# attention_2: transposes of the probability rows three units behind the scores instead of two

## What is computed

```python
x = layer_norm(image_embeds, ln1_g, ln1_b)      # 32 context tokens
l = layer_norm(latents, ln2_g, ln2_b)           # 512 tokens
q = l @ Wq
kv = jnp.concatenate([x, l], axis=1) @ Wkv      # 544 keys and values
w = jax.nn.softmax(einsum('bhqd,bhkd->bhqk', q * scale, k * scale), axis=-1)
out = einsum('bhqk,bhkd->bhqd', w, v)
return out @ Wo
```

## Time and profile before

| | |
|---|---|
| median of three executions | 2352.45 us (2346.61 to 2354.46) |
| profiled execution | 2344.8 us, of which the span is 2343.0 us |
| TensorE matmul busy | 1963.6 us (84%) |
| TensorE weight loads busy | 1245.7 us (53%) |
| VectorE, ScalarE, GpSimd busy | 1222.7 us (52%), 927.0 us (40%), 799.1 us (34%) |
| mean granted TensorE clock | 0.908 of full speed |
| longest wait in total | GpSimd L1213 for VectorE L1398, 313.2 us over 128 times |

### The profile page before, as it was taken

The page is one execution under the profiler, slowest core; times in us unless marked ns, Lnnn a source line. Parts: engine busy times, 40 slices in busy tenths (PEclk is TensorE's granted clock), DMA queues, the critical chain, the costliest instruction groups (busy, mean ns, idle before and its releaser), DMA issues. The chain is left out here.

```text
span 2343.0 us, 32200 instructions
## 1 busy us (share of the span) xinstructions
PE 1963.6 (84%) x11205; PEld 1245.7 (53%) x11205; DVE 1222.7 (52%) x3078; ACT 927.0 (40%) x2061; POOL 799.1 (34%) x959
## 2 busy tenths in 40 slices
PE   3379799887969999887979989887888899887589
PEld 3246456554746556554655646544565556544255
DVE  3338656443676546453576636454385446454344
ACT  0135255253532455253542445435442155344121
POOL 0135356342440136443351126443250036353000
PEclk9569899998989999998989989989898999999689
DMA  5020000002030000000112000000203000000030
GB/s 200 20 79 1 1 1 2 1 1 73 1 113 2 5 1 1 1 1 12 62 32 84 1 5 1 1 1 1 73 1 108 5 1 2 1 1 1 0 108 5
DMA packets 32304, 59.09 MB, mean 25 GB/s; under 512 B 6160, under 2 KB 10512, under 8 KB 30992
## 3 DMA queue, kind: packets, MB, share of 16 engines
q1 hardware_dynamic: 32144, 57.03, 6.9%
HBM read 53.86 MB, written 3.16 MB: 24 GB/s over the span
## 5 line engine op out<-in xcount | busy, mean ns | idle before, releaser
L1213 POOL TENSOR_TENSOR rows<-rows,rinv 128x512 f32<-128x512 f32 x256 | 261.1, 1041 | 313.2 <-DVE rinv L1398 313.2
L1393 DVE TENSOR_REDUCE nmax<-psum 128x2 f32<-128x1088 f32 x128 | 165.2, 1290 | 124.8 <-PE psum L1263 124.8
L1480 POOL TENSOR_TENSOR rows<-rows,rinv 128x256 f32<-128x256 f32 (+3 forms) x128 | 159.3, 1254 | 198.4 <-DVE rinv L1617 198.4
L1354 ACT ACTIVATE rows<-psum,nmax 128x544 f32<-128x544 f32 x256 | 180.6, 710 | 49.5 <-DVE nmax L1393 49.4
L1984 ACT ACTIVATE region_b<-psum 128x512 f32<-128x512 f32 x132 | 78.8, 597 | 255.2 <-PE psum L1931 255.1
L2025 DVE TENSOR_TENSOR region_b<-region_b,psum 128x512 f32<-128x512 f32 x128 | 87.9, 687 | 159.1 <-PE psum L1955 154.6
L1273 PE MATMUL psum<-weights,rows 128*128 128x128 f32 x1024 | 163.0, 282 | 7.6 <-ACT turned L1361 4.1
L1257 PE MATMUL psum<-region_a,region_b 64*128 64x256 f32 x1024 | 160.9, 406 | 9.7 <-ACT rows L1354 6.0
L1955 PEld LDWEIGHTS psum<-region_c,region_b 128*128 128x128 f32 x1024 | 134.0, 192 | 45.3 <-DVE region_b L2028 26.2
L1528 PE MATMUL psum<-weights,rows 128*128 128x128 f32 x640 | 107.0, 294 | 58.9 <-POOL rows L1480 48.1
L1575 ACT ACTIVATE rows<-psum,nmax 128x128 f32<-128x128 f32 (+3 forms) x256 | 132.6, 524 | 55.8 <-DVE nmax L1612 55.8
(11 more groups left out here) (434 smaller groups left out, 3771.0 us busy)
## 6 DMA issues: line engine op xcount, KB each, us to landing
region_a<-w_centred SPq DMA_DIRECT2D x32, 258.0 KB, 5.0
region_a<-in_w SPq DMA_DIRECT2D x32, 256.0 KB, 4.6
region_a<-in_eg SPq DMA_DIRECT2D x32, 256.0 KB, 5.7
region_a<-in_eu SPq DMA_DIRECT2D x32, 256.0 KB, 5.9
region_c<-in_weights SPq DMA_DIRECT2D x32, 256.0 KB, 6.8
weights<-in_weights SPq DMA_DIRECT2D x4, 1264.5 KB, 9.3
w_centred<-region_a SPq DMA_DIRECT2D x1, 2064.0 KB, 6.3
region_a<-in_w SPq DMA_DIRECT2D x1, 2048.0 KB, 22.2
```

The lines of the kernel that those rows point to most:

```text
L1213: nc.gpsimd.tensor_tensor(row, row, rinv[:, 2 * u + j:2 * u + j + 1].broadcast_to([P, S]), ALU.mult).then_inc(done, 1)
L1354: nc.scalar.activation(heads_of(u, j), scores_of(u, j), ACT.Exp, bias=nmax[:, 2 * u + j:2 * u + j + 1], accum_out=psum_of[:, 2 * u + j:2 * ...
L1393: nc.vector.tensor_reduce(nmax[:, 2 * u:2 * u + 2], both_scores(u), AX.X, ALU.max, negate=True).then_inc(s.mx, 1)
L1480: nc.gpsimd.tensor_tensor(rows, rows, over(rinv[:, 2 * u:2 * u + 2], 2, [P, 2, keys(u)]), ALU.mult).then_inc(s.pn, 1)
```

## The change

`LAG` becomes 3: at each step the turned unit is s-3 instead of s-2, on TensorE, ScalarE and VectorE, and `values` is for v = s-5. The loop has one step more. A fourth buffer of probability rows is laid over `xn` and `xnt` (made one tile of 1088 columns instead of two of 512), which are free by then. The waits are renumbered to match, and the transposed context part goes to `ctx_bank(u)` instead of `ctx_bank(u + 1)`: at step s that is `ctx_bank(s-3)` instead of `ctx_bank(s-1)`, which is the same bank.

```diff
-        xn = sb("xn", [P, T, D])
-        xnt = sb("xnt", [P, S])
+        norm_rows = sb("norm_rows", [P, 2 * NK2])
+        xn, xnt = part(norm_rows, 0, [P, T, D]), part(norm_rows, T * D, [P, S])
...
-            LAG = 2
+            LAG = 3
...
+            def rows_of(u):
+                return prob2[:, u % 4, :] if u % 4 < 3 else norm_rows[:, :]
...
-                        if u >= 3:
-                            pe.wait_ge(s.cc, u - 2)
+                        if u >= 4:
+                            pe.wait_ge(s.cc, u - 3)
...
                     def turn_ctx(u):
                         pe.wait_ge(s.pnc, u + 1)
-                        pe.wait_ge(s.ex, 2 * min(u + 2, units))
-                        nc.tensor.transpose(bank(ctx_bank(u + 1))[0:2 * K, P:2 * P], ctx_of(u), ident[:, :]).then_inc(s.tc, 1)
+                        pe.wait_ge(s.ex, 2 * min(u + 3, units))
+                        nc.tensor.transpose(bank(ctx_bank(u))[0:2 * K, P:2 * P], ctx_of(u), ident[:, :]).then_inc(s.tc, 1)
...
-                    for step in range(units + 5):
-                        v = step - 4
-                        if step >= 8 and step % 4 == 0:
+                    for step in range(units + 6):
+                        v = step - 5
+                        if step >= 9 and step % 4 == 1:
                             context(step // T - 2)
...
-                        if j == 0 and u >= 3:
-                            act.wait_ge(s.tb, u - 2)
-                            act.wait_ge(s.tc, u - 2)
+                        if j == 0 and u >= 4:
+                            act.wait_ge(s.tb, u - 3)
+                            act.wait_ge(s.tc, u - 3)
...
-                    for step in range(units + 5):
-                        if step >= 8 and step % 4 == 0:
+                    for step in range(units + 6):
+                        if step >= 9 and step % 4 == 1:
                             copy_heads(step // T - 2)
...
                         nc.vector.tensor_copy(ctx2[0:2 * K, p % 2, P * t:P * (t + 1)],
-                                              bank(ctx_bank(u + 1))[0:2 * K, P:2 * P]).then_inc(s.cc, 1)
-
-                    for step in range(units + 4):
+                                              bank(ctx_bank(u))[0:2 * K, P:2 * P]).then_inc(s.cc, 1)
+
+                    for step in range(units + LAG + 1):
```

More of the change, by code:

```diff
@@ L1181, in both_scores @@
                 return bass.AP(psum, lo, [[8 * 512, P], [NK2 + 448, 2], [1, NK2]])
+            def rows_of(u):
+                return prob2[:, u % 4, :] if u % 4 < 3 else norm_rows[:, :]
             def heads_of(u, j):
-                return prob2[:, u % 3, NK2 * j:NK2 * (j + 1)]
+                return rows_of(u)[:, NK2 * j:NK2 * (j + 1)]
             def keys_of(u, j):
                 lo = (NK2 + K) * j
-                return prob2[:, u % 3, lo:lo + S]
+                return rows_of(u)[:, lo:lo + S]
             def ctx_of(u):
-                return prob2[:, u % 3, S:S + 2 * K]
+                return rows_of(u)[:, S:S + 2 * K]
             def turned_to(u, j):
```

## The result

The changed kernel takes 2374.86 us in the median of four executions (2371.0 to 2376.68), against 2352.59 for the kernel before: ratio 1.0091, 95% interval 1.0066 to 1.0116, slower by about 22 us. The forecast was 9.6 us more (2362), with a range for 8 in 10 from 2355 to 2369. The sign was right, the forecast size less than half of the measured one.

A forecast was written before the change was run, and what follows sets the result against it. It took TensorE's own work to bound the middle of the loop, with waits only at start and end. -4.06 (start) + 12.84 (end) + 0.8 (clock) = 9.6 us on 2352.45 gave 2362.0 us; 8 in 10 range 2355 to 2369.

The forecast's parts named there:

- The middle: 0: Middle of the loop: TensorE's own work sets the pace and GpSimd's wait is not the last, so 0 us.
- Rival A: Middle of the loop: hidden waits for GpSimd's rows that a fourth buffer would cure, giving 2346 us; 5%.
- The end: +12.84 us: End of the loop: one more step without scores, with a third bare copy, 3.21 us in each of four blocks.
- The start by dependencies: scores(2) to scores(5) in 10.27 us: Start of the loop: earlier scores, paced by the exponentials, 10.27 us in all four blocks; together 4.06 us gained.
- The clock at the start: +0.8 us: Steps 2 and 3: longer waits may halve TensorE's clock; 0.8 us allowed in one block of four, bounds 0 and 8.
- rival C: Start of most blocks: half clock where TensorE is last, 4 to 8 us on top of 8.8, giving 2365 to 2369; 15%.
- the clock halves over steps 3 to 5: Start of the loop: half clock over these steps was listed as a sign that the prediction is wrong; no size given.
- Other stages: 0: Outside the block: no term; the median's 7.65 us above the profiled execution was put down to nothing this block shows.

The follow-up runs named there:

- after_again: The changed kernel, unchanged, timed and profiled a second time; ratio 1.0105 to the kernel before.
- after_bank: The changed kernel with the first transposes of units 29 and 31 written to bank 0 instead of bank 6; ratio 1.0086 to the kernel before.
- after_warm3: The changed kernel with 3, 3 and 1 extra matmuls behind the scores of steps 1, 2 and 3, where TensorE idled; ratio 1.0054 to the kernel before.
- before_warm: The kernel before with 6 extra matmuls behind the scores of step 1, where TensorE idled; ratio 1.0034.
- before_end: The kernel before with a shorter loop end: turn(31, 0) into bank 0, turn(31, 1) ahead of step 33's values, output projection started earlier; ratio 0.9992.
- layout_only: The kernel before with only xn and xnt merged into one tile, LAG still 2 and three row buffers; ratio 1.0002.
- the two delays: The kernel before with 1.8 or 3.4 us of useless matmuls per block between loop and output projection; ratios 1.0027 and 1.0056.
- delay_34: The kernel before with 3.4 us of useless matmuls per block between loop and output projection; ratio 1.0056.
- shorter_34: The kernel before with before_end's shorter end, 3 extra matmuls in step 1, and scores(0) started before the last copies of the values' context part; ratio 0.9943.
- after_raster: The changed kernel with after_warm3's extra matmuls and 0.86 us more of them before the output projection; ratio 1.0074 to the kernel before.
- after_shifted: The changed kernel with after_warm3's extra matmuls and 1.67 us more of them before the output projection; ratio 1.0080 to the kernel before.
- end_warm3: The kernel before with before_end's shorter end and 3 extra matmuls in step 1; ratio 0.9961.
- same_again: The kernel before, unchanged, run for a second profile; it took 2352.3 us.
- before_warm3: The kernel before with 3 extra matmuls in the idle 1.49 us of step 1; ratio 1.0007.

## Why the prediction was right or wrong

- *The middle: 0.* Right: 98.33 us in both, to the hundredth. (Only in after_again and after_bank did one loop of four come to 99.3 to 99.4 us, when the half clock of a start lasted into it.) Rival A (hidden waits) is out. With it goes, here, the reading that the Trainium skill's rule suggested (Perfetto Trace Analysis, Identifying the Most-Contended Engine and Optimization Strategy). The weight loads were 64% busy, yet a fourth buffer found no bubble to fill; the trace disagrees with that use of the rule.
- *The end: +12.84 us.* Right: 4 x 3.22 = 12.9, with the third bare copy where it was put. after_bank shows that the bare copies are part of it: two copies less took 1.56 us off each end.
- *The start by dependencies: scores(2) to scores(5) in 10.27 us.* Right, 10.26, where the clock is full (after_warm3).
- *The clock at the start: +0.8 us.* This term was mis-sized, and it is the first step that failed. It measured (15.51 - 14.68) x 2 + (17.57 - 14.68) x 2 = 7.4 us, the upper bound of 8 almost. Its words were "most of it is hidden by the waits; I allow 0.8 us in one block of four". It carried a price over from blocks in which the half clock fell on a step with slack, and left out that the change takes work out of the very steps in which TensorE idles, so that two idle times of 1.4 to 1.5 us now follow each other (in the third and fourth loop; in the first two the clock fell right behind the first one, as before, and stayed down longer). That idle time is what halves the clock is shown by after_warm3, which fills both and keeps it full; filling only one of them was not tried. Instead of giving back 4.06 us the starts took 3.35. In the mechanism that was rival C, given 15%, and "the clock halves over steps 3 to 5" was one of the prediction's own signs of being wrong; C's 2365 to 2369 was still too low for the reason in the next item.
- *Other stages: 0.* This step failed too; it was not even put, beyond "from nothing that this block shows". Some 5 to 7 us of the loss lie outside `attention_2` (5.2 and 7.1 in the two timings, of which only the second is clear of zero by its interval). That they come with a block that begins or ends at another time, and not with the new order of work, is supported, not proven. For it: before_warm (+8.2) and before_end (+7.0) have LAG 2 and pay the same, layout_only pays nothing, and the length of `attention_2f` follows its start in nearly all profiles. Against a simple rule stand the two delays, which pay nothing. So the cause of this part stays open. Five kernels were given a block length that was to bring back the 128.9 us (delay_34, shorter_34, after_raster, after_shifted, end_warm3); of their 15 `attention_2f` four had it. One reason is in the traces: the part of `attention_2` ahead of the loop takes 27.3 to 28.8 us within one profile of the kernel before (same_again), so the length of a block is not set by the edit alone.

Sum of the two: (7.4 - 0.8) + 6.1 us make the 12.7 between 9.6 and 22.3; the 6.1 is what is left of 22.3 after the loops' 16.2.

## What to carry to other kernels

Before a pipeline is made deeper, ask for the wait that it would loosen. Where none is in the trace, the depth can only cost, at the end (each added step without its cover, 3.2 us here) and at the start. Work taken out of a filling pipeline left TensorE idle here, and the clock that this costs is to be priced on the steps in which TensorE is last, at twice their time, and not by what it cost where waits hid it. Look for gains at the two ends instead: free banks for the last transposes, an early start and three useless matmuls in an idle 1.5 us together made this kernel 0.6% faster (shorter_34; the three matmuls alone gave nothing in the median, 1.0007).

## What was not expected of the hardware

A change confined to one block can be lost outside it, where the instructions are the same: before_end gained 8.9 us in its loops and 1.9 in all, before_warm gained 0.2 and lost 8. `attention_2f` took 128.9 to 133.7 us within one execution of one kernel, as the half clock fell on different steps. Lengthening a block by 0.3 us (before_warm against before_warm3, 128.9 and 128.6 us) cost some 5 us elsewhere, though the two intervals meet (1.0019 and 1.0020) and don't make this firm; lengthening it by 1.9 or 3.6 us cost nothing elsewhere that the timings can tell. With TensorE kept busy in step 1 the clock stayed full through the loop in all 32 loops of the eight kernels that did so; in the others it halved in 23 of 36.
